# A decoder kernel on one core: the last routed selection overlapped with the routed network, the third ternary matrix made within it

## What is computed

```python
x = x + _L0_attn_ref(_layernorm(x), ...)       # a Mamba mixer: projections, chunked scan, output product
x = x + _L0_xattn_ref(_layernorm(x), ctx, mask)  # recall from memory tokens, softmax
x = x + _L0_ffn_ref(_layernorm(x), ...)        # routed network, below
x = x + _L1_attn_ref(_layernorm(x), ...)       # attention over the 4 batch entries of a position
x = x + _L1_xattn_ref(_layernorm(x), ctx)      # product with ctx in fp8 steps
x = x + _L1_ffn_ref(_layernorm(x), w1, w2, w3) # ternary weights, 8-bit activations
```

```python
weights = jnp.einsum('bsd,do->bso', x, W_r).squeeze(-1) + b_r
topk_vals, topk_idx = jax.lax.top_k(weights, K)          # K = 128 of 512 rows, per batch entry
sel_mask = weights > threshold[:, None]
xg = jnp.take_along_axis(x, topk_idx[..., None], axis=1)
h = jax.nn.gelu(jnp.einsum('bkd,df->bkf', xg, W1) + b1)  # 2048 hidden columns
blk = jnp.einsum('bkf,fd->bkd', h, W2) + b2
vals = blk * (wg * gate)[..., None]                      # scattered back onto the rows
return processed + x * (~sel_mask)[..., None]
```

## Time and profile before

| | us |
|---|---|
| median of 3 runs (1101.0 to 1102.41) | 1101.39 |
| the profiled execution | 1102.29 |
| its span, first to last instruction | 1100.6 |
| TensorE busy | 1050.0 |
| VectorE busy | 846.6 |
| ScalarE busy | 639.5 |
| POOL busy | 480.3 |

### The profile page before, as it was taken

How to read it: one execution, slowest core, us unless ns; L and a number is a source line. 1 busy time by engine, 2 the same in 40 slices (tenths; PEclk the granted TensorE clock), 3 DMA queues, 4 the chain that set the end, 5 groups by cost and what they waited for, 6 DMA issues and landing times.

```text
span 1100.6 us, 15542 instructions
## 1 busy us (share of the span) xinstructions
PE 1050.0 (95%) x5255; PEld 785.1 (71%) x5255; DVE 846.6 (77%) x1612; ACT 639.5 (58%) x1243; POOL 480.3 (44%) x727
## 2 busy tenths in 40 slices
PE   7999999999999999999999999998899999999898
PEld 6777888788878888766566777776676666666544
DVE  6787766776677767846988758858888988978975
ACT  5643444344444443336566547663468889888784
POOL 8343324332433323425888513205654554644520
PEclk9999999999999999999999999999999999999999
DMA  8300000000000000217010035420001211212122
GB/s 292 113 1 1 1 1 1 1 1 1 1 1 1 1 1 1 80 47 301 34 39 1 1 129 185 151 93 1 1 6 24 34 37 33 51 33 51 33 55 75
DMA packets 46446, 52.48 MB, mean 48 GB/s; under 512 B 32544, under 2 KB 33568, under 8 KB 44064
## 3 DMA queue, kind: packets, MB, share of 16 engines
q1 hardware_dynamic: 46368, 51.49, 14.8%
HBM read 39.92 MB, written 4.19 MB: 40 GB/s over the span
## 4 chain that ended last, share of the span: by engine, by line
PE 59%; DVE 17%; POOL 11%; issue 6%; ACT 6%; DMA 1%; POOLq 0%; DVEq 0%; ACTq 0%
PE bank L422 44%; PE bank L520 3%; PE bank L430 3%; PE bank L870 3%; DVE cum_h L992 1%; PE bank L511 1%; PE bank L531 1%; DVE half_lo L1362 1%; DVE prod L1484 1%; POOL wq L2492 1%; PE bank L781 1%; PE bank L501 1%; POOL wq L2488 1%; DVE wgt L1000 1%; DVE y L1028 1%
## 5 line engine op out<-in xcount | busy, mean ns | idle before, releaser
L422 PE MATMUL bank<-win_hi,a_uT_hi 128*128 128x512 f32 (+1 forms) x320 | 126.0, 394 | 5.8 <-DVE win_lo L943 3.1
L422 PE MATMUL bank<-win_lo,a_uT_hi 128*128 128x512 f32 (+1 forms) x320 | 119.7, 374 | 0.0
L422 PE MATMUL bank<-win_hi,a_uT_lo 128*128 128x512 f32 (+1 forms) x320 | 119.4, 373 | 0.0
L1761 ACT ACTIVATE ex<-bank 128x48 f32<-128x48 f32 x16 | 3.4, 210 | 144.5 <-PE bank L475 144.5
L2356 POOL TENSOR_TENSOR y<-y,off 128x512 f32<-128x512 f32 x24 | 38.1, 1587 | 106.1 <-DVE off L1013 106.1
L422 PEld LDWEIGHTS bank<-win_hi,a_uT_hi 128*128 128x128 f32 x320 | 60.3, 188 | 19.5 <-issue 3.9
L422 PEld LDWEIGHTS bank<-win_lo,a_uT_hi 128*128 128x128 f32 x320 | 60.3, 188 | 12.4 <-issue 2.4
L422 PEld LDWEIGHTS bank<-win_hi,a_uT_lo 128*128 128x128 f32 x320 | 60.2, 188 | 11.3
L520 PEld LDWEIGHTS bank<-xs,wgt 128*128 128x128 f32 x512 | 61.1, 192 | 7.7 <-issue 5.7
L422 PE MATMUL bank<-wq,eT 128*128 128x512 f32 x128 | 58.8, 602 | 6.5 <-ACT eT L2095 6.5
L422 PE MATMUL bank<-f,fqT_next 128*128 128x512 fp8e4 (+1 forms) x312 | 64.0, 362 | 0.0
(11 more groups left out here) (358 smaller groups left out, 3203.2 us busy)
## 6 DMA issues: line engine op xcount, KB each, us to landing
wchunk<-w_in SPq DMA_DIRECT2D x32, 256.0 KB, 4.8
stage<-f_in SPq DMA_DIRECT2D x4, 1408.0 KB, 6.6
x<-x_in SPq DMA_DIRECT2D x16, 256.0 KB, 6.2
land<-win_in SPq DMA_DIRECT2D x4, 1024.0 KB, 8.8
wq<-ctxT_in SPq DMA_DIRECT2D x4, 1024.0 KB, 6.2
out<-x SPq DMA_DIRECT2D x16, 256.0 KB, 2.0
ctx<-ctx_in SPq DMA_DIRECT2D x3, 1024.0 KB, 4.8
first_stage<-f_in SPq DMA_DIRECT2D x2, 1408.0 KB, 14.2
```

The costliest lines, as they stand in the source:

```text
L422: made = e.matmul(bank, a, b, start=start and n == 0, stop=stop and n == len(pairs) - 1)
```

## The change

- Mixer: sums makes only the parts that are used (sums_of), and the third part of ex, the decay over the whole tile, is the product of the first two, made by POOL (whole_decay) in tiles with c = 1, 2. decay_state waits for y_off instead of ex_ready.
- Selection: keep_row and wrow are gone, select reads the bank. Places come from four bf16 products of 4, 3, 2 and 1 columns on before_b and ones_b; the additions on VectorE, and the subtraction of 1, are gone (count starts at 1).
- Last selection: for hidden tiles 0 and 1 the products with the selected rows of batch entries 0 to 2 (384 columns) come early (early_up), with gelu, hT_lo and down of tile 0 for them; late_up and low_h_part do the last 128 columns. Filler there goes from 19, 19 and 5 products to 7, 3 and 5.
- Memory: half of the last quarter of wq is made by POOL within the last steps of the loop.
- Ternary: the third matrix goes to last_stage (a place of its own) and to the first half of stage, is loaded at tiles 7 and 11, summed from tile 9 on and made in tiles 12 to 15. The first is made from tile 1 on.
- Attention: routed additions 0 and 1 stand ahead of both wqkv_lo, 2 and 3 behind low_du(0); banks that aren't accumulators are claimed first.

```diff
+        def sums_of(m):
+
+
+            c = m % TPB
+            return range(0 if c else 1, 2 if c < TPB - 1 else 1)
...
-                e.matmul(bank[:, 0:NH], upto_r[:].bitcast(F32), logs, start=True, stop=True)
-                e.matmul(bank[:, NH:2 * NH], beyond[:], logs, start=True, stop=True)
-                e.matmul(bank[:, 2 * NH:3 * NH], ones[:].broadcast_to([P, P]), logs, start=True, stop=True).then_inc(
-                    sig("sums_done"), 1)
+                for n in sums_of(m):
+                    made = e.matmul(bank[:, n * NH:(n + 1) * NH], (upto_r[:].bitcast(F32), beyond[:])[n], logs, start=True,
+                                    stop=True)
+                made.then_inc(sig("sums_done"), 1)
...
-                bank = banks.claim(w, ("pos", b), "route_step", 7 * b + 6)
-                w.wait_ge("consts", 10)
-                keep_busy(bank, 19 if b == BATCH - 1 else 3)
-                w.wait_ge("route_step", 7 * b + 5)
-                e.matmul(bank[:, 0:TPB], before[:], route[b][:, 4, :], start=True, stop=False)
-                e.matmul(bank[:, 0:TPB], ones[:].broadcast_to([P, P]), route[b][:, 5, :], start=False, stop=True).then_inc(
-                    sig("route_turn"), 1)
+                bank = banks.claim(w, ("pos", b), "route_step", 3 * b + 3)
+                keep_busy(bank, 5 if b == BATCH - 1 else 3)
+                w.wait_ge("route_step", 3 * b + 2)
+                sel = selected(b)
+                made = e.matmul(bank[:, 0:TPB], before_b[:], sel, start=True, stop=False)
+                for c in range(1, TPB):
+                    made = e.matmul(bank[:, c:TPB], ones_b[:].broadcast_to([P, P]), sel[:, 0:TPB - c], start=False,
+                                    stop=c == TPB - 1)
+                made.then_inc(sig("route_turn"), 1)
...
+            def early_up(f):
+                bank = banks.claim(w, ("early", f), "hT_hi", f + 1)
+                if f == 0:
+                    keep_busy(bank, 7)
+                w.wait_ge("gathered_lo", BATCH - 1)
+                w.wait_ge("half_lo_0", f + 1)
+                hi, lo = half_hi[0][f % 2], half_lo[0][f % 2]
+                pairs = []
+                for k in range(KD):
+                    cols = slice(k * P, (k + 1) * P)
+                    pairs += thrice(hi[:, cols], lo[:, cols], gathered_hi[:, k, first_slots], gathered_lo[:, k, first_slots])
+                product(bank[:, first_slots], pairs).then_inc(sig("early_up"), 1)
+
+            def late_up(f):
+                bank = banks.of["early", f]
+                hi, lo = half_hi[0][f % 2], half_lo[0][f % 2]
+                tiles = [slice(k * P, (k + 1) * P) for k in range(KD)]
+                w.wait_ge("route_kept", 2 * BATCH - 1)
+                product(bank[:, last_slots], [(half[:, tiles[k]], gathered_hi[:, k, last_slots])
+                                              for k in range(KD) for half in (hi, lo)], stop=False)
+                w.wait_ge("gathered_lo", BATCH)
+                product(bank[:, last_slots], [(hi[:, tiles[k]], gathered_lo[:, k, last_slots]) for k in range(KD)],
+                        start=False).then_inc(sig("up_done"), 1)
+
+            def down_part(f, b):
+                slots = slice(b * SLOTS, (b + 1) * SLOTS)
+                return product(accs[b][:], thrice(hT_hi[f % 2][:, slots], hT_lo[f % 2][:, slots],
+                                                  half_hi[1][f % 2][:], half_lo[1][f % 2][:]),
+                               start=f == 0, stop=f == KF - 1)
+
+            def early_down(b):
+                w.wait_ge("early_h_lo", 1)
+                w.wait_ge("half_lo_1", 1)
+                down_part(0, b)
...
+                if n == NT + 3:
+                    early_up(0)
                 if t4 is not None:
                     spread_weights(t4)
+                if n == NT + 4:
+                    early_up(1)
+                    accs = [banks.claim(w, ("acc", b), "blk_ready", b + 1) for b in range(BATCH)]
+                    banks.set_aside([k for k in range(8) if banks.banks[k] in accs])
                 if t2 is not None:
                     spread_tops(t2)
                 if t0 is not None:
                     turn_u(t0)
+                if n == NT + 5:
+                    early_down(0)
+                    early_down(1)
                 if t6 is not None:
                     gather(t6)
                 if t5 is not None:
                     positions(t5)
-
-            accs = [banks.claim(w, ("acc", b), "blk_ready", b + 1) for b in range(BATCH)]
-            banks.use([n for n in range(8) if banks.banks[n] not in accs])
+            early_down(2)
...
-                w.wait_ge("route_kept", 3 * b + 1)
+                w.wait_ge("route_turn", 4 * b + 1)
...
-                    made = e.tensor_scalar(spare[:], wrow[:], wc[:, c:c + 1], None, ALU.is_ge, ALU.add,
+                    made = e.tensor_scalar(spare[:], banks.of["row", b][:], wc[:, c:c + 1], None, ALU.is_ge, ALU.add,
                                            accum_out=cnt[:, c:c + 1])
...
-                w.wait_ge("route_step", 7 * b + 1)
-                e.memset(acc[:, 0:1], 0.0)
-                e.tensor_scalar(sel, cnt, SLOTS - 0.5, None, ALU.is_lt).then_inc(sig("route_step"), 1)
-                for c in range(1, TPB):
-                    w.wait_ge("route_step", 7 * b + 1 + c)
-                    e.tensor_tensor(acc[:, c:c + 1], acc[:, c - 1:c], sel[:, c - 1:c], ALU.add).then_inc(
-                        sig("route_step"), 1)
+                w.wait_ge("route_step", 3 * b + 1)
+                e.tensor_scalar(selected(b), cnt, SLOTS - 0.5, None, ALU.is_lt).then_inc(sig("route_step"), 1)
...
                 if n == NT + 4:
-                    low_half(0, 0)
+                    w.wait_ge("early_h", 1)
+                    low_h_part(first_slots, "early_h_lo")
                 if t5 is not None:
                     pick_slots(t5)
+                if n == NT + 4:
+                    memory_magic(BATCH - 1, 0)
...
-                if n == NT + 4:
+                if n == NT + 2:
+                    low_half(0, 0)
+                    low_half(0, 1)
                     low_half(1, 0)
...
-                if f in (4, 6):
-                    memory_magic(BATCH - 1, f // 2 - 2)
-                if f in (0, 7, 14):
-                    ternary_scale((0, 7, 14).index(f))
-                for n, first in enumerate((0, 7, 14)):
+                if f == 5:
+                    memory_magic(BATCH - 1, 1)
+                if f in (1, 7, 12):
+                    ternary_scale((1, 7, 12).index(f))
+                for n, first in enumerate((1, 7, 12)):
...
                 if n == 0:
+                    add_routed(0)
+                    add_routed(1)
                     low_qkv(0)
-                if n < len(scattered_by) - 1:
+                if n == 1:
+                    low_du(0)
+                    add_routed(2)
+                    add_routed(3)
+                if 0 < n < len(scattered_by) - 1:
...
-                if 1 <= n < 3:
-                    ternary_part(2, QUARTERS - 3 + n)
...
+            def whole_decay(m):
+
+                if m % TPB in (0, TPB - 1):
+                    return
+                up, rest, whole = (ex[m % 2][:, k, :] for k in range(3))
+                w.wait_ge("ex_ready", m + 1)
+                w.wait_ge("state_decayed", decay_count(m - 1))
+                e.tensor_tensor(whole, up, rest, ALU.mult)
...
+                if n == NT + 5:
+                    scale_up(BATCH - 1, 0)
+                if n == NT + 6:
+                    round_add(BATCH - 1, 0)
+                    round_off(BATCH - 1, 0)
+                    scale_down(BATCH - 1, 0)
...
-                if f in (12, 14):
-                    load_stage(2, f // 2 - 6)
+                if f in (7, 11):
+                    load_stage(2, (7, 11).index(f))
+            w.wait_ge("ternary", 2 * QUARTERS + QUARTERS // 2)
             e.dma_start(wproj[:], wproj_in).then_inc(sig("w_loaded"), 16)
```

167 lines of the change are left out of this document (98 added, 69 removed).

## The result

The changed kernel takes 1087.34 us (median of four runs, 1086.49 to 1088.0), the kernel before 1101.9 us in the same session (1101.0 to 1102.51). The ratio is 0.9868 with a 95% interval of 0.9851 to 0.9885, that is 12.7 to 16.4 us less. Forecast were 1086.2 us and a saving of 15.2 us. The profiled execution of the changed kernel took 1088.0 us, with a span of 1086.2 us.

A forecast was written before the change was run, and what follows sets the result against it. TensorE, busy 95% of the span, was taken as the bound, full in the mixer, idle at the routed network's end and attention's start. 4.2 + 0.5 + 5.5 + 1.0 + 4.0 = 15.2 us off 1101.39 gives 1086.2; range 1082 to 1095.

The forecast's parts named there:

- Mixer: Decay sums in the mixer: 24 small products less at 0.22 us, 5.3 us, of which 4.2 taken (1.0 to 5.3).
- the prediction's own sign: Mixer: the last tile's sums start 3.5 to 4.5 us sooner; moved by less than 2 us, the prediction is wrong.
- where TensorE waits for un: Mixer: 0.2 us of the saving from fewer small products is lost at TensorE's waits for un.
- gains given back: Rival: VectorE and POOL close behind TensorE; mixer gives 1.0, attention start 1.5, saving 8.5 us: 1092.9 us; chance 0.27.
- not waiting as the prediction says: End of the mixer: the clock's fall to 0.50 from 472 to 474 us lies where TensorE waits.
- First three selections: Selections of the first three batches: copy on ScalarE, serial additions and -1 on VectorE go; 0.5 us (0 to 1.5).
- Last selection: Last recall to hidden tile 2: early products replace filler, the shorter chain is offset by POOL; 5.5 us (3.5 to 7.2).
- The rival without a meeting: Last selection: the router dot product and POOL's scale_up don't meet at the shared port; 1084.8 us, chance 0.13.
- Rest of the routed network: Hidden tiles 2 to 15: waits of TensorE, one from ScalarE's stage DMA wait, shrink; 1.0 us (0 to 1.6).
- Attention's start: Routed network's end and first attention tiles: 1.5 us from free banks first, 2.5 of 3.7 us waits; 4.0 (1.5 to 5.2).
- Late next: Attention's start: low_du(0) is late next, behind two routed additions, and the second half of qkv(0) waits for their bank.
- the slower rival: The clock falls in the last selection and stays, to 1.2 GHz for four hidden tiles: 1107.0 us; chance 0.03.

The follow-up runs named there:

- first profile: Profiled execution of the changed kernel in the main result, with a low granted clock at 40 us: 1088.0 us, span 1086.2 us.
- second profile: Profile of the changed kernel run again with no edit: median 1086.14 us, ratio 0.9857 to the kernel before, span 1084.3 us.
- mixer_alone: The kernel before with only the mixer part of the change (24 small products less): 1101.11 us over twelve runs, ratio 0.9992.
- before_state_last: The kernel before, all three small products kept, with VectorE's state additions moved behind un and cT: 1099.37 us, ratio 0.9975 to the kernel before.
- state_last: The changed kernel with VectorE's state additions in the mixer moved behind un and cT: 1086.75 us, ratio 0.9873 to the kernel before.
- no_overlap: The changed kernel with the early work of hidden tiles 0 and 1 moved back behind the last gather, filler restored: 1094.28 us, ratio 0.9929.
- qkv_later: The changed kernel with both wqkv_lo of VectorE waiting for POOL's norm factor of the first attention tile: 1086.99 us, ratio 0.9881.
- stage_undone: The changed kernel with the third ternary matrix loaded as before and its last two quarters made in the attention: 1095.7 us, ratio 0.994.

## Why the prediction was right, and where its terms were off

The time and the sign came as forecast, the last selection is the largest part and the attention's start the next. That the sum came this close is in part luck: the mixer's term was 2.3 us too large, and against it stand up to 1.4, 0.4 and 0.7 us in three terms that were too small and 1.1 us that no term had.

- **Mixer**, 4.2 us forecast, 1.9 measured. By the prediction's own sign this part was wrong: the last tile's sums start at 457.85 in the first profile and at 456.38 in the second, against 458.17 before, so 0.3 (behind the low clock at 40 us) and 1.8 us sooner and not 3.5 to 4.5; under 2 us was to mean that it is wrong. The price of a product was right where it stands: 0.22 us. The step that failed is that only 0.2 us were set off "where TensorE waits for un". The earlier trace rows show 1.3 us of idle time in 100 us, and I took this as a sign that nothing else is near. The trace of before has waits of 0.81 us for un in the tiles with c = 2; a product taken away in front of such a wait gives nothing. In the tiles with c = 3 there was no wait listed, and all of the 0.44 us went into a new one. Part of the rival "gains given back" was true: VectorE is close behind, by its order and not by its load. Another 1.1 us, from the last zs to the first recall, came by a way that the forecast did not have: the fall of the clock at the mixer's end lies at 471 to 474.5 us in the trace of the kernel before, where TensorE is busy for 2.00 of 2.00 us, and not waiting as the prediction says. In all thirteen other traces, mixer_alone and before_state_last among them, it begins between 457 and 464, ahead of TensorE's last wait for wgt, and in the second profile that wait is 0.27 us (at 468.17) where it was 1.37 (at 469.38). With one trace of the kernel before it stays open whether the change or the execution moved the fall. The twelve runs of mixer_alone, 2.1 us less at most, leave little room for it beside the 1.9 of the stretch. And where the fall lasted 6.8 us (state_last, no_overlap, qkv_later) this part took 51.6 us again.
- **First three selections**, 0.5 forecast (0 to 1.5), 1.9 measured. From one turn of the weights to the next it was 37.20 and 37.80 us, and is 36.78 and 36.77 in the second profile, 36.77 and 37.25 in the first. The three traces with the old selection have 127.7 to 127.9 us between the recalls, the eleven with the new one 125.8 or 126.3: so 1.4 or 1.9 us, and what sets the 0.5 between the two is not known. The cheaper products for the places and the copy that is gone are the two candidates. No run tells them apart, and this stays open.
- **Last selection**, 5.5 forecast, 5.9 measured, and the working held in its steps. The dot product met POOL's multiply: 1.52 us in place of 0.69. A part of the 1.5 us that the forecast set down came from elsewhere: POOL's route factor took 0.89 us instead of 0.26 beside half_lo. Together these are 1.46 us. Comparisons from a bank took 0.75 us. Short products took 2.94 us for 24 (2.8 forecast), those of 384 columns 4.4 us (4.2). The gather started at 637.40 in the first profile and at 635.45 in the second, 2.5 and 4.5 us sooner (some 5 forecast, the savings ahead of it); hidden tile 2 at 646.03 and 644.1, 8.6 and 10.6 us sooner. The clock stayed at 1.00 there. The rival without a meeting was tried by itself and is 0.8 us faster, where the forecast had 1.4 between them (and 1.7 in the high end of this term).
- **Rest of the routed network**, 1.0 forecast (0 to 1.6), 1.7 measured, just above its bound. ScalarE's 2.50 us wait for a stage DMA is gone, and of TensorE's three waits in the tiles one of 0.26 us is left. Undoing the load (stage_undone) gives back 1.0.
- **Attention's start**, 4.0 forecast, 4.0 measured. The banks give 1.97 (1.5 forecast), the order of the additions 0.1 to 0.2. The other 1.9 are put down to the quarters that are gone by what is left over, and no run measures them alone. No idle time stands before turn_du(2), and qkv(1) waits 0.31 us, not 2.13. Late next was not low_du(0) but the first turn of d_u, with 1.04 us.

That the clock could take more than the terms was the slower rival. It did not come in the last selection, but stage_undone shows its mechanism at another place: a wait of 4.30 us, and 6.8 us at 1.2 GHz from its end part on. The clock came back there too.
